# Ten bf16 conversions of a two-layer block move from ScalarE to GpSimd, in a hand-ordered attention loop

## Chip, cores and metric

The kernel runs on one core of one Trainium2 chip. The metric is the device time of one execution in microseconds (us). Work is spread over five engines that run their own instruction lists in order and meet only at semaphores: TensorE (PE in the profile, with its weight loads as PEld), VectorE (DVE), ScalarE (ACT), GpSimd (POOL) and SyncE (SP, which here only issues transfers).

## The reference, cut to what matters

```
x = x + tanh(g_xattn[0]) * L0_xattn(ctx, ctx, layernorm(x))     # long convolution
x = x + tanh(g_ffn[0])   * L0_ffn(layernorm(x))                 # dense + routed LoRA
x = x + tanh(g_xattn[1]) * L1_xattn(layernorm(x), ctx, ...)     # attention, 16 heads of 16
x = x + tanh(g_ffn[1])   * L1_ffn(layernorm(x), ...)            # 8 experts + shared one

def qdq(x):                                   # per row, to 8 bits and back
    s = max(max(abs(x), axis=-1) / 127, 1e-8)
    return clip(round(x / s), -127, 127) * s

def L1_xattn(x, cond, ...):
    q = qdq(x) @ qdq(wq).T + bq
    k, v = split(cond @ wkv.T + bkv)
    o = softmax(q k / sqrt(16)) v
    return qdq(o) @ qdq(wp).T + bp
```

x is 8 blocks of 128 rows by 256. The change concerns the third line alone, at the two places where a row is rounded (qdq(x) and qdq(o)).

## The kernel before, in words

Every engine has one list of instructions, written out by hand as loops over a stage number s. A block b is one of the 8 batches. The attention is a software pipeline of eight stages (s = 0 to 7) and a tail: in stage s the engines work on blocks s+3, s+2, s+1, s-1, s-2, s-3 and s-5 at different depths.

A row is rounded in two steps. VectorE multiplies by the reciprocal of the scale and adds 1.5 * 2^23, which leaves the integer in the low bits of the fp32 number. Then ScalarE subtracts that constant again and writes the small integer as bf16, which is exact. For the rows that go into the query projection the first step is the last one of `a_quant(b)` (line 1013, buffer AT_) and the second is `a_zq_(b)` (line 620, buffer AQ). For the attention outputs they are the last step of `o_norm(b)` (line 1055, buffer OT_) and `o_q_(b)` (line 661, buffer OQ).

What surrounds these two steps in a stage s, engine by engine, in the order of the lists:

- VectorE: maximum of the scores of block s (line 1022, two), the subtraction (line 1032, two), then `o_norm(s-2)` and `a_quant(s+3)` interleaved (lines 1042 to 1055 and 1002 to 1013), `m_rows(s-5)` (line 1073), `m_stats(s-4)` (line 1066).
- ScalarE: `a_zt_(s+2)` (line 624), exponential of quarter 0 of block s-1 (line 651), `m_rstd(s-5)` (lines 549 and 552), `o_q_(s-3)`, `a_q0_(s+2)` (line 630), exponential 1, `a_last_subtract(s)` (line 646, four), `a_q_(s+2)` (line 636), `a_rstd(s+3)` (lines 549 and 552), exponentials 2 and 3, `o_ev_(s-3)` (line 675), `a_zq_(s+3)`, `o_y_(s-3)` (line 670), `o_pe_(s-1)` (line 657), `m_zt_(s-5)` (line 685).
- TensorE: `a_turn(s-1, 0)` (line 1494), `a_transpose(s+2)` (line 1441), which waits for AQ and, for blocks 6 and 7, for `o_y_` of blocks 0 and 1, since both use PSUM bank 6; `o_rows(s-2)` (line 1519), `a_project(s+2)` (line 1447), `a_turn(s-1, 1)`, `a_q_transpose(s+2)` (line 1454), `a_turn(s-1, 2)` and `(s-1, 3)`, `a_scores(s+1)` (line 1480), which waits for the subtraction of block s on both engines, `o_transpose(s-3)` (line 1534), values (line 1510), `o_project(s-3)` (line 1540), values, `m_transpose(s-5)` (line 1587).
- GpSimd: for block b = 2 to 7 the masked keys of `block_keys(b)` (line 472, two), then, from b = 5, `finish(b-5)` (lines 482 and 484), which scales the attention's output and adds it to the residual. `finish` waits for `o_y_`. After block 7 come `finish(3)` and `finish(4)`. Blocks 5 to 7 are finished by VectorE.

After the attention the experts run: 16 units of matmuls (lines 1648 and 1666) with the transposing transfers of SyncE between them.

Of the kernel before, what the change touches and what calls it, by code (L numbers as in the profile page):

```python
# [23 lines left out]
ALU = mybir.AluOpType  # L24
# [5 lines left out]
NB = 8  # L30
# [12 lines left out]
ROUND = 1.5 * 2.0 ** 23  # L43
# [29 lines left out]
def build(nc, x, ctxr, kern, consts, rows, cols, wff, bt, wkv, wqp, gate, w1, w3, w2, sw1, sw3, sw2, out):  # L73
    with ExitStack() as ctx:
# [48 lines left out]
        def carve(region, at=0):  # L123
# [184 lines left out]
            "e_si",  # L308
            "e_ht",
            "e_acc"))  # L310
        e_xa, e_xd = sem("e_xa"), sem("e_xd")
        e_td = [sem("e_td%d" % n) for n in range(XS)]
        x4, stored = sem("x4"), sem("stored")
# [5 lines left out]
        AZT = 5  # L319
# [114 lines left out]
        @block.gpsimd  # L434
        def _(pool):
            nc.gpsimd.memset(ONES[:, :], 1.0).then_inc(ones_s, 1)
            nc.gpsimd.memset(EPSC[:, :], EPS).then_inc(ones_s, 1)
            nc.gpsimd.memset(GL[:, :, :], FULL).then_inc(ones_s, 1)
            pool.wait_ge(L["kern"], 16)
            nc.gpsimd.tensor_tensor(KP[:, P - 1:P], KP[:, P - 1:P], KP[:, 383:384], ALU.add).then_inc(lag0, 1)  # L440
            pool.wait_ge(L["ctx"], 16)
            for h in range(NH0):
                if not dve_has(h):
                    if h >= RING:
                        pool.wait_ge(conv, h - RING + 1)
                    if h == 3:
                        pool.wait_ge(nmr, 2)
                    upper(nc.gpsimd, h).then_inc(kv_p, 1)
                    lower(nc.gpsimd, h).then_inc(kv_p, 1)
            pool.wait_ge(conv, NH0)  # L450
            nc.gpsimd.memset(V[:, :, :, 16:17], 1.0).then_inc(v_ones, 1)
            nc.gpsimd.memset(V[:, :, :, 17:VW], 0.0).then_inc(v_ones, 1)

            def bias_values(b):

                pool.wait_ge(vev, b + 1)
                v = V[:, b, :, 0:HD1]
                nc.gpsimd.tensor_tensor(v, v, ROW[:, BV_AT:BV_AT + DM].rearrange("p (h d) -> p h d", h=NH1), ALU.add  # L458
                                        ).then_inc(v_b, 1)

            def block_keys(b):

                if b == 0:
                    pool.wait_ge(kev, 2)
                if b == GT:
                    pool.wait_ge(kev, 2 * NG)
                if b == 2:
                    pool.wait_ge(a_s0, 2)
                elif b > 2:
                    pool.wait_ge(a_s, b - 2)  # L470
                for c in range(2):
                    nc.gpsimd.tensor_tensor(KBD[:, b % 2, c], KT[:, c, b, :].unsqueeze(1).to_broadcast([P, 2, P]),  # L472
                                            MASK.unsqueeze(2).to_broadcast([P, 2, P]), ALU.mult).then_inc(kbd, 1)

            def bias_rows(b):
                pool.wait_ge(x2, b + 1)
                nc.gpsimd.tensor_tensor(XPB[:, b, :], X[:, b, :], BPG[:, :], ALU.add).then_inc(xpb, 1)

            def finish(b):

                pool.wait_ge(o_y, b + 1)
                nc.gpsimd.tensor_tensor(Y[:, b % 2, :], Y[:, b % 2, :], SWPB[:, :], ALU.mult).then_inc(o_sc, 1)  # L482
                pool.wait_ge(o_sc, b + 1)
                nc.gpsimd.tensor_tensor(X[:, b, :], Y[:, b % 2, :], XPB[:, b, :], ALU.add).then_inc(x3, 1)

            def expert_rows(u):

                g, e = divmod(u, NE)
                pool.wait_ge(m_gt, gates_done(g))
                if u == 0:  # L490
                    pool.wait_ge(a_et, 4 * NB)
                if u >= XS:
                    pool.wait_ge(e_td[u % XS], 16 * (u // XS))
                for j in range(2):
                    b = GT * g + j
                    nc.gpsimd.tensor_scalar(XB[:, u % XS, j, :], MX[:, b, :], GG[:, b, e:e + 1], 1.0,  # L496
                                            ALU.mult, ALU.mult).then_inc(e_xb, 1)


            def fold_sums(b):  # L500

                pool.wait_ge(prod, 3 * NH0)
                pair = PR[:, :, :, :, :].rearrange("p (a b) i h j -> p b a (i h j)", a=NL)[:, b]
                nc.gpsimd.tensor_tensor(pair[:, :, 0:512], pair[:, :, 0:512], pair[:, :, 512:1024], ALU.add  # L504
                                        ).then_inc(fold, 1)

            fold_sums(FOLD0)
            bias_values(0)
            fold_sums(FOLD0 + 1)
            for b in range(1, NB - 2):  # L510
                bias_values(b)
                if b + FOLD0 + 1 < NB:
                    fold_sums(b + FOLD0 + 1)
            pool.wait_ge(prep, PREP)
            pool.wait_ge(isum, NB)
            block_keys(0)
            bias_values(NB - 2)
            bias_values(NB - 1)
            block_keys(1)
            for b in range(NB - 2):  # L520
                bias_rows(b)
            pool.wait_ge(v_dg, 3)
            for b in range(2, NB):
                block_keys(b)
                if b < 4:
                    bias_rows(b + NB - 4)
                if b >= 5:
                    finish(b - 5)
            for b in range(NB - 5, NB - LATE):
                finish(b)  # L530
            expert_rows(0)
            expert_rows(1)
            for u in range(2, NG * NE):
                expert_rows(u)

        @block.scalar
        def _(act):
# [120 lines left out]

            def o_q_(b):
                act.wait_ge(o_n, ONT * (b + 1))  # L660
                nc.scalar.activation(OQ[:, b % 2, :], OT_[:, b % 2, :], ACT.Copy, bias=-ROUND).then_inc(o_q, 1)

            def o_y_(b):
# [61 lines left out]
            for s in range(NB):  # L725
                if s + 2 < NB:
                    a_zt_(s + 2)
                if s >= 1:
                    a_exp(s - 1, 0)
                if s >= 5:  # L730
                    m_rstd(s - 5)
                if s >= 3:
                    o_q_(s - 3)
                if s + 2 < NB:
                    a_q0_(s + 2)
                if s >= 1:
                    a_exp(s - 1, 1)
                a_last_subtract(s)
                if s + 2 < NB:
                    a_q_(s + 2)  # L740
                if 1 <= s < NB - 3:
                    a_rstd(s + 3)
                if s >= 1:
                    a_exp(s - 1, 2)
                    a_exp(s - 1, 3)
                if s >= 3:
                    o_ev_(s - 3)
                if s + 3 < NB:
                    a_zq_(s + 3)
                if s >= 3:  # L750
                    o_y_(s - 3)
                if s >= 1:
                    o_pe_(s - 1)
                if s >= 5:
                    m_zt_(s - 5)
# [66 lines left out]
        def _(dve):  # L822
# [173 lines left out]
            def a_quant(b, k):  # L996

                a, s = b % 2, s_az
                s.wait()
                if k == 0:  # L1000
                    dve.wait_ge(a_rs, 2 * (b + 1))
                    s.mark(V_.tensor_scalar(AZ[:, a, :], X[:, b, :], MV[:, b, 0:1], RS[:, b:b + 1],
                                            ALU.subtract, ALU.mult))
                elif k == 1:
                    s.mark(V_.tensor_reduce(AM[:, b:b + 1], AZ[:, a, :], AX.X, ALU.max, apply_absolute_value=True))
                elif k == 2:
                    s.mark(V_.tensor_scalar(AS[:, b:b + 1], AM[:, b:b + 1], 1.0 / QMAX, SMIN, ALU.mult, ALU.max))
                elif k == 3:
                    s.mark(V_.reciprocal(AR[:, b:b + 1], AS[:, b:b + 1]))
                else:  # L1010
                    if b >= 2:
                        dve.wait_ge(a_zq, b - 1)
                    s.mark(V_.tensor_scalar(AT_[:, a, :], AZ[:, a, :], AR[:, b:b + 1], ROUND, ALU.mult, ALU.add))

# [20 lines left out]
            def o_norm(b, k):  # L1035
# [14 lines left out]
                elif k == 4:  # L1050
                    s.mark(V_.reciprocal(OR[:, b:b + 1], OS[:, b:b + 1]))
                else:
                    if b >= 2:
                        dve.wait_ge(o_q, b - 1)
                    s.mark(V_.tensor_scalar(OT_[:, a, :], O[:, a, :], OR[:, b:b + 1], ROUND, ALU.mult, ALU.add))


# [227 lines left out]
        def _(pe):  # L1285
# [148 lines left out]


            def a_transpose(b):
                pe.wait_ge(a_zq, b + 1)
                chain_free(b - 2)
                for k in range(NL):
                    at = 64 * k  # L1440
# [79 lines left out]
                ins.then_inc(o_nt, 1)  # L1520

            def o_transpose(b):
                pe.wait_ge(o_q, b + 1)
                if b + 5 < NB:
                    pe.wait_ge(a_q, 2 * (b + 6))
                elif b < NB - LATE:
# [234 lines left out]
```

## Time and profile before

| | |
|---|---|
| median of 3 runs | 219.73 us (219.03 to 220.08) |
| profiled execution, time | 218.84 us |
| profiled execution, span | 216.7 us, so 2.14 us lie around the span |
| mean granted TensorE clock | 0.965 |
| busy in the span: PE, DVE, ACT, POOL | 176.3, 164.2, 108.5, 81.5 us |

The span is what the profiler sees between the first and the last instruction; the time of a run also holds what lies around it. The attention loop takes from about 105 to 163 us of the span.

### The profile page before, as it was taken

How to read it: one execution, taken by the hardware profiler on the slowest of the kernel's cores; microseconds unless marked ns; L12 is line 12 of the kernel's file. 1: busy time of each engine (PE TensorE's matmuls, PEld its weight loads, DVE VectorE, ACT ScalarE, POOL GpSimd, SP SyncE). 2: the span in 40 equal slices, each digit the busy share in tenths (PEclk: the TensorE clock that was granted, in tenths of full speed). 3: DMA queues.
4: the chain of work that ended last, by engine and by line, in shares of the span. 5: the costliest groups of instructions: out<-in, count | busy, mean ns of one | idle time of the engine just before them, and what ended most of it. 6: DMA issues, size and time to landing. Idle time of an engine off the chain costs nothing.

```text
span 216.7 us, 3606 instructions
## 1 busy us (share of the span) xinstructions
PE 176.3 (81%) x1156; PEld 111.4 (51%) x1156; DVE 164.2 (76%) x465; ACT 108.5 (50%) x288; POOL 81.5 (38%) x114
## 2 busy tenths in 40 slices
PE   0369999989989989885788788798787959979962
PEld 0236555558555556542455556565566327636531
DVE  0698999994178999979689999999936853575634
ACT  2440343211423245641588789887975473543621
POOL 1386557024755550593121204420220373065100
PEclk9999999999999999999599999999999788999998
DMA  6989970000000000000000000000000057665772
GB/s 182 395 208 374 363 258 15 3 0 0 0 0 2 3 0 2 0 0 2 3 0 0 5 0 5 3 0 0 3 0 3 2 97 145 76 120 113 161 164 97
DMA packets 22625, 15.17 MB, mean 70 GB/s; under 512 B 17648, under 2 KB 21328, under 8 KB 22096
## 3 DMA queue, kind: packets, MB, share of 16 engines
q1 hardware_dynamic: 21968, 13.94, 24.1%
q10 hardware_dynamic: 640, 1.02, 1.3%
q8 instruction: 9, 0.15, 0.3%
q14 instruction: 8, 0.07, 0.1%
HBM read 9.68 MB, written 1.07 MB: 50 GB/s over the span
## 4 chain that ended last, share of the span: by engine, by line
PE 50%; DVE 18%; ACT 12%; DMA 7%; issue 7%; SPq 4%; DVEq 0%
PE PS L1648 7%; PE PS L1316 5%; PE PS L1318 5%; PE PS L1317 5%; DMA X<-x 4%; PE PS L1404 4%; PE PS L1666 3%; PE PS L1380 3%; DMA R<-R 3%; SPq L426 3%; PE PS L1338 3%; ACT R L651 3%; ACT R L646 2%; PE PS L1480 2%; PE PS L1347 2%
## 5 line engine op out<-in xcount | busy, mean ns | idle before, releaser
L496 POOL TENSOR_SCALAR R<-QT,SM 128x256 bf16<-128x256 f32 x32 | 15.8, 508 | 28.0 <-DVE SM L1100 19.6
L1269 DVE TENSOR_TENSOR R<-R,PS 128x512 bf16<-128x512 f32 (+1 forms) x17 | 11.7, 687 | 15.4 <-ACT R L773 8.1
L1022 DVE TENSOR_REDUCE SM<-PS 128x8 f32<-128x1024 f32 x16 | 18.8, 1213 | 3.0 <-PE PS L1480 1.9
L1648 PE MATMUL PS<-R 128*128 128x512 bf16 x64 | 17.1, 388 | 3.6 <-DMA R<-R 3.6
L1494 PE MATMUL PS<-CON,R 128*128 128x128 f32 x128 | 19.0, 281 | 1.2 <-ACT R L651 1.2
L472 POOL TENSOR_TENSOR R<-R,CON 128x256 f32<-128x256 f32 x16 | 9.6, 620 | 24.7 <-PE PS L1480 15.5
L651 ACT ACTIVATE R<-PS 128x512 f32<-128x512 f32 x32 | 18.4, 600 | 0.9 <-PE PS L1494 0.8
L337 POOL TENSOR_TENSOR R<-CT 128x512 f32<-128x512 f32 x12 | 13.8, 1154 | 12.2 <-PE PS L1318 6.7
L773 ACT ACTIVATE R<-PS 128x512 f32<-128x512 f32 x17 | 10.1, 596 | 14.8 <-PE PS L1648 14.8
L549 ACT ACTIVATE LNV<-MV,EPSC 128x1 f32<-128x1 f32 (+1 forms) x26 | 7.6, 293 | 17.6 <-DVE MV L945 11.2
L1494 PEld LDWEIGHTS PS<-CON,R 128*128 128x128 f32 x128 | 14.5, 143 | 3.5 <-issue 3.0
L1316 PE MATMUL PS<-R,T_R 128*128 128x384 f32 x32 | 13.8, 514 | 2.1 <-DVE T_R L837 2.1
L1666 PE MATMUL PS<-R 128*128 128x256 bf16 (+1 forms) x80 | 14.5, 309 | 0.2 <-DVE R L1257 0.2
L1032 DVE TENSOR_TENSOR R<-PS,SM 128x1024 f32<-128x1024 f32 (+1 forms) x16 | 14.6, 947 | 0.0
L482 POOL TENSOR_TENSOR T_R<-T_R,SWPB 128x256 f32<-128x256 f32 x5 | 3.6, 728 | 27.9 <-ACT T_R L670 27.9
L504 POOL TENSOR_TENSOR R<-R 128x1024 f32<-128x1024 f32 x6 | 14.1, 2353 | 0.0
L1317 PE MATMUL PS<-R,T_R 128*128 128x384 f32 x32 | 13.6, 509 | 0.0
L1318 PE MATMUL PS<-R,T_R 128*128 128x384 f32 x32 | 13.6, 509 | 0.0
L1404 PE MATMUL PS<-WFF,T_R 128*128 128x352 f32 x32 | 11.4, 480 | 2.5 <-ACT T_R L600 2.1
L1666 PEld LDWEIGHTS PS<-R 128*128 128x128 bf16 (+1 forms) x80 | 10.0, 127 | 6.0 <-DVE R L1269 1.4
L570 ACT CAST R<-WST 128x2048 bf16<-128x2048 f32 x3 | 5.7, 1900 | 12.9 <-DMA WST<-w 12.9
L458 POOL TENSOR_TENSOR R<-R,ROW 128x256 f32<-128x256 f32 x8 | 6.1, 767 | 15.1 <-ACT R L591 15.0
(152 smaller groups left out, 428.1 us busy)
## 6 DMA issues: line engine op xcount, KB each, us to landing
WST<-w SPq DMA_DIRECT2D x3, 1024.0 KB, 11.3
T_R<-lagged SPq DMA_DIRECT2D x2, 768.0 KB, 7.7
X<-x SPq DMA_DIRECT2D x2, 512.0 KB, 6.9
CT<-ctxr SPq DMA_DIRECT2D x1, 1024.0 KB, 7.5
y<-X SPq DMA_DIRECT2D x8, 128.0 KB, 1.9
WKV<-wkv SPq DMA_DIRECT2D x1, 512.0 KB, 9.9
WQP<-wqp ACTq DMA_DIRECT2D x1, 512.0 KB, 6.2
R<-sw SPq DMA_DIRECT2D x3, 128.0 KB, 4.4
```

The source lines that it names most:

```text
L496: nc.gpsimd.tensor_scalar(XB[:, u % XS, j, :], MX[:, b, :], GG[:, b, e:e + 1], 1.0, ALU.mult, ALU.mult).then_inc(e_xb, 1)
L504: nc.gpsimd.tensor_tensor(pair[:, :, 0:512], pair[:, :, 0:512], pair[:, :, 512:1024], ALU.add).then_inc(fold, 1)
L651: nc.scalar.activation(ET[:, b % 2, 4 * k:4 * k + 4, :], PS[:, 4 + k % 2, :].rearrange("p (h n) -> p h n", h=4), ACT.Exp).then_inc(a_ex, 1)
L1022: V_.tensor_reduce(MX1[:, b % 2, 8 * c:8 * c + 8], S4[:, 8 * c:8 * c + 8, :], AX.X, ALU.max, negate=True).then_inc(a_mx, 1)
L1032: V_.tensor_tensor(SS[:, a, ks, :], S4[:, ks, :], MX1[:, a, ks].unsqueeze(2).to_broadcast([P, n, P]), ALU.add).then_inc(a_sub, 1)
L1316: M(one, T[:, h, 0:P], kv[:, 0:NB], start=True, stop=True)
L1317: M(two, T[:, h, P:2 * P], kv[:, 0:NB], start=True, stop=False)
L1318: M(two, T[:, h, 0:P], kv[:, NB:2 * NB], start=False, stop=True).then_inc(conv, 1)
L1404: ins = M(PS[:, 6 + b % 2, 0:352], FZT[:, b % 2, k, :], WFF[:, k, :], start=(k == 0), stop=(k == NL - 1))
L1494: ins = TR(PS[:, 4 + k % 2, P * h:P * h + P], SS[:, b % 2, 4 * k + h, :], I)
L1648: ins = M(PS[:, 2 + 2 * (v % 2) + n, :], lhs, rhs, start=(k == 0), stop=(k == NL - 1))
L1666: ins = M(acc(g, j), src[:, P * j:P * j + P], W2[:, e - 1, :] if e >= 1 else SW2, start=(e == 0 and j % 2 == 0), stop=(e == NE), skip_grou ...
```

## The change

GpSimd gets two new steps. `rounded_rows(b)` does for blocks 3 to 7 what `a_zq_(b)` did, and `rounded_out(b)` for blocks 0 to 4 what `o_q_(b)` did: the same subtraction of the constant with bf16 output, as a `tensor_scalar`. Two semaphores, a_zp and o_qp, count them; the waits of VectorE (buffer free again) and TensorE (rows ready) follow. ScalarE keeps the rows of blocks 0 to 2 and the outputs of blocks 5 to 7.

```diff
+            def rounded_rows(b):
+
+                pool.wait_ge(a_z, AZT * (b + 1))
+                pool.wait_ge(a_tr, b - 1)
+                nc.gpsimd.tensor_scalar(AQ[:, b % 2, :], AT_[:, b % 2, :], -ROUND, None, ALU.add).then_inc(a_zp, 1)
+
+            def rounded_out(b):
+
+                pool.wait_ge(o_n, ONT * (b + 1))
+                if b >= 2:
+                    pool.wait_ge(o_tr, b - 1)
+                nc.gpsimd.tensor_scalar(OQ[:, b % 2, :], OT_[:, b % 2, :], -ROUND, None, ALU.add).then_inc(o_qp, 1)
...
             for b in range(2, NB):
+                if b >= 3:
+                    rounded_rows(b)
+                if b >= 5:
+                    rounded_out(b - 5)
                 block_keys(b)
                 if b < 4:
                     bias_rows(b + NB - 4)
                 if b >= 5:
                     finish(b - 5)
             for b in range(NB - 5, NB - LATE):
+                rounded_out(b)
                 finish(b)
...
             def o_q_(b):
                 act.wait_ge(o_n, ONT * (b + 1))
+                if b == NB - LATE:
+                    act.wait_ge(o_tr, b - 1)
...
-                if s >= 3:
-                    o_q_(s - 3)
                 if s + 2 < NB:
                     a_q0_(s + 2)
...
-                if s + 3 < NB:
-                    a_zq_(s + 3)
                 if s >= 3:
                     o_y_(s - 3)
...
-                    if b >= 2:
+                    if b >= 5:
+                        dve.wait_ge(a_zp, b - 4)
+                    elif b >= 2:
                         dve.wait_ge(a_zq, b - 1)
...
-                    if b >= 2:
-                        dve.wait_ge(o_q, b - 1)
+                    if b == NB - 1:
+                        dve.wait_ge(o_q, 1)
+                    elif b >= 2:
+                        dve.wait_ge(o_qp, b - 1)
...
             def a_transpose(b):
-                pe.wait_ge(a_zq, b + 1)
+                if b < 3:
+                    pe.wait_ge(a_zq, b + 1)
+                else:
+                    pe.wait_ge(a_zp, b - 2)
...
             def o_transpose(b):
-                pe.wait_ge(o_q, b + 1)
+                if b < NB - LATE:
+                    pe.wait_ge(o_qp, b + 1)
+                else:
+                    pe.wait_ge(o_q, b - (NB - LATE) + 1)
```

The first place is GpSimd's list from the keys of block 5 on. Before, it reads as follows (line 472 the keys, 482 and 484 `finish` of blocks 0 and 1; in brackets the semaphores that a row waits for):

```order
L472 TENSOR_TENSOR R<-R,CON 128x256 [waits a_s]
L472 TENSOR_TENSOR R<-R,CON 128x256
L482 TENSOR_TENSOR T_R<-T_R,SWPB 128x256 [waits o_y]
L484 TENSOR_TENSOR X<-T_R,R 128x256 [waits o_sc]
L472 TENSOR_TENSOR R<-R,CON 128x256 [waits a_s]
```

In the changed kernel the same stretch holds the new steps (line 491 `rounded_rows`, 498 `rounded_out`; 473, 483 and 485 are the old 472, 482 and 484). It begins with the rows of block 5:

```order
L491 TENSOR_SCALAR R<-R 128x256 [waits a_tr,a_z]
L498 TENSOR_SCALAR R<-R 128x256 [waits o_n]
L473 TENSOR_TENSOR R<-R,CON 128x256 [waits a_s]
L473 TENSOR_TENSOR R<-R,CON 128x256
L483 TENSOR_TENSOR T_R<-T_R,SWPB 128x256 [waits o_y]
L485 TENSOR_TENSOR X<-T_R,R 128x256 [waits o_sc]
L491 TENSOR_SCALAR R<-R 128x256 [waits a_tr,a_z]
L498 TENSOR_SCALAR R<-R 128x256 [waits o_n]
```

The last two rows are the rows of block 6 and the outputs of block 1. They stand behind `finish(0)`, which waits for ScalarE's `o_y_(0)`. In the same way the rows of block 7 stand behind `finish(1)`.

The second place is ScalarE's list at the end of stage 4 and the start of stage 5. Before (line 675 `o_ev_(1)`, 620 `a_zq_(7)`, 670 `o_y_(1)`, 657 `o_pe_(3)`, 624 `a_zt_(7)`, 651 exponential 0 of block 4, 549 and 552 `m_rstd(0)`, 661 `o_q_(2)`, 630 `a_q0_(7)`):

```order
L675 COPY R<-PS 128x256 [waits o_tr]
L620 ACTIVATE R<-R 128x256 [waits a_z]
L670 ACTIVATE T_R<-PS,SM 128x256 [waits o_mm]
L657 COPY T_R<-PS 128x512 [waits a_pv]
L624 COPY R<-PS 128x256 [waits a_tr]
L651 ACTIVATE R<-PS 128x512 [waits a_et]
L549 ACTIVATE LNV<-MV,EPSC 128x1 [waits m_ln]
L552 ACTIVATE RS<-LNV 128x1 [waits m_rs]
L661 ACTIVATE R<-R 128x256 [waits o_n]
L630 ACTIVATE T_R<-PS,SM 128x256 [waits a_mm]
```

In the changed kernel (the line numbers are 18 to 21 higher):

```order
L696 COPY R<-PS 128x256 [waits o_tr]
L691 ACTIVATE T_R<-PS,SM 128x256 [waits o_mm]
L676 COPY T_R<-PS 128x512 [waits a_pv]
L643 COPY R<-PS 128x256 [waits a_tr]
L670 ACTIVATE R<-PS 128x512 [waits a_et]
L568 ACTIVATE LNV<-MV,EPSC 128x1 [waits m_ln]
L571 ACTIVATE RS<-LNV 128x1 [waits m_rs]
L649 ACTIVATE T_R<-PS,SM 128x256 [waits a_mm]
```

The two conversions, old lines 620 and 661, are gone from between the others, and with the first of them ScalarE's wait for VectorE's a_z.

## Rows read from the trace of the kernel before

**Rows 1.** Page, part 1: busy time, share of the span and instructions by engine.

```profile
PE 176.3 (81%) x1156; PEld 111.4 (51%) x1156; DVE 164.2 (76%) x465; ACT 108.5 (50%) x288; POOL 81.5 (38%) x114
```

**Rows 2.** Windows of stages 4, 5, 7: length; busy PE, PEld, DVE, ACT, POOL.

```profile
129.70:137.20 7.50, 6.26 (x85) 4.42 (x78) 7.43 (x20) 6.62 (x19) 2.61 (x4) 1.00 0.01 3
137.20:143.80 6.60, 5.34 (x68) 3.88 (x60) 6.43 (x14) 6.44 (x19) 2.60 (x4) 1.00 0.01 2
...
150.40:157.00 6.60, 5.07 (x75) 3.64 (x72) 6.43 (x14) 5.72 (x16) 1.46 (x2) 1.00 0.01 2
```

**Rows 3.** Chain that ended last, in order of time: start, length, what.

```profile
136.96 0.35 DVE R L1013
137.33 0.42 ACT R L620
...
146.91 0.40 ACT R L661
...
153.75 0.40 ACT R L661
```

**Rows 4.** Timeline of ScalarE: start, length, instruction, idle time ahead and its releaser.

```profile
129.78 0.42 ACT L620 ACTIVATE R<-R 128x256 bf16<-128x256 f32 x1 [0.98 <-DVE R L1013]
130.10 0.46 ACT L670 ACTIVATE T_R<-PS,SM 128x256 f32<-128x256 f32 x1
...
134.99 0.20 ACT L552 ACTIVATE RS<-LNV 128x1 f32<-128x1 f32 x1
...
139.65 0.20 ACT L552 ACTIVATE RS<-LNV 128x1 f32<-128x1 f32 x1
139.76 0.40 ACT L661 ACTIVATE R<-R 128x256 bf16<-128x256 f32 x1
```

**Rows 5.** Timeline of GpSimd.

```profile
120.33 1.23 POOL L472 TENSOR_TENSOR R<-R,CON 128x256 f32<-128x256 f32 x2 [5.65 <-PE PS L1480]
130.64 0.73 POOL L482 TENSOR_TENSOR T_R<-T_R,SWPB 128x256 f32<-128x256 f32 x1 [9.08 <-ACT T_R L670]
131.44 0.74 POOL L484 TENSOR_TENSOR X<-T_R,R 128x256 f32<-128x256 f32 x1
132.14 1.19 POOL L472 TENSOR_TENSOR R<-R,CON 128x256 f32<-128x256 f32 x2
```

**Rows 6.** Timeline of TensorE.

```profile
128.86 0.39 PE L1540 MATMUL PS<-R 128*128 128x256 bf16 x2 [0.21 <-ACT R L675]
...
130.70 0.27 PE L1441 MATMUL PS<-IDB,R 128*128 128x128 bf16 x2 [0.29 <-ACT T_R L670]
...
134.22 1.15 PE L1480 MATMUL PS<-R 32*128 32x256 f32 x16 [0.30 <-ACT R L646]
...
136.48 0.39 PE L1540 MATMUL PS<-R 128*128 128x256 bf16 x2 [0.33 <-ACT R L675]
...
138.25 0.27 PE L1441 MATMUL PS<-IDB,R 128*128 128x128 bf16 x2 [0.22 <-ACT T_R L670]
```

**Rows 7.** Timeline of VectorE.

```profile
120.35 0.75 DVE L1002 TENSOR_SCALAR R<-X,MV,RS 128x256 f32<-128x256 f32 x1
...
135.30 0.41 DVE L1002 TENSOR_SCALAR R<-X,MV,RS 128x256 f32<-128x256 f32 x1
```

**Rows 8.** Groups by line: the GpSimd conversion to bf16 in the experts.

```profile
L496 POOL TENSOR_SCALAR R<-QT,SM 128x256 bf16<-128x256 f32 x32 | 15.8, 508 | 28.0 <-DVE SM L1100 19.6 <-DMA R<-R 8.4
```

**Rows 9.** Timeline of TensorE: longest idle times after 20 us, scores of block 1.

```profile
101.17 0.30 PE L1410 MATMUL PS<-CON,T_R 128*64 128x128 f32 x1 [1.43 <-DVE T_R L977]
...
105.61 2.09 PE L1480 MATMUL PS<-R 32*128 32x256 f32 x16 [0.44 <-ACT R L646]
...
175.51 0.44 PE L1587 MATMUL PS<-CON,QT 128*128 128x128 f32 x2 [1.48 <-DVE QT L1073]
```

**Rows 10.** Windows behind them: the granted clock is the third number from the end.

```profile
103.00:104.00 1.00, 0.61 (x2) 0.13 (x2) 1.00 (x3) 0.30 (x2) 0.00 (x0) 0.50 0.00 0
...
178.00:179.00 1.00, 1.00 (x5) 0.58 (x3) 0.00 (x0) 0.70 (x3) 0.80 (x2) 0.50 0.00 0
```

More of the change, by code:

```diff
@@ L310, in build @@
             "e_acc"))
+        a_zp, o_qp = sem("a_zp"), sem("o_qp")
         e_xa, e_xd = sem("e_xa"), sem("e_xd")
```

## Prediction

> **What bounds the kernel now.** I read the page first, then windows by stage, then the chain that ended last, then the timelines of each engine from 120 to 160 us. The page alone misleads: ScalarE is busy for half of the span only [rows 1]. But in the attention loop nearly everything is full. In stage 4 VectorE is busy 7.43 of 7.50 us, and in stage 5 ScalarE and VectorE are both busy 6.4 of 6.6 us [rows 2]. The chain shows a hand-over inside this loop. Up to 137.3 us it runs along VectorE, the last piece being the rounding of block 7 (line 1013). At 137.33 it goes to ScalarE's conversion of the same rows, and from there to the end of the attention it alternates between ScalarE and TensorE; the conversions of outputs are pieces of it at 146.91 and 153.75 [rows 3], and the one at 139.76 lies on it as well [rows 4]. So ScalarE's conversions cost something only from stage 4's end on. Before that VectorE sets the pace and ScalarE waits for it: 0.98 us ahead of the conversion of block 6 [rows 4].
>
> **What the change removes.** Five conversions of 0.42 us (rows) and five of about 0.40 us (outputs) leave ScalarE, some 4.1 us of busy time. Instructions overlap a little there: a conversion started at 129.78 and its follower at 130.10, so one is worth 0.32 us of ScalarE's time [rows 4]. On the chain lie the outputs of blocks 2, 3 and 4, three times 0.31 (139.76 follows at 0.11 after the line before, whose result it does not need), hence **0.93 us given back**, if nothing else moves. The conversion of block 7 is on the chain too, but its work does not go away: TensorE still waits for it, now from GpSimd.
>
> **What it adds.** Ten conversions on GpSimd. The trace has no GpSimd conversion with a constant. The nearest row is the experts' one-input operation of the same shape and output type, 0.51 us [rows 8]. Its lower bound is ScalarE's own 0.42 [rows 4], its upper bound the two-input operation of 0.73 [rows 5]. I take 0.50. By the first of these a conversion is 0.1 us slower than today, which alone is nothing.
>
> **The order on GpSimd is the costly part.** The rows of block 6 stand behind `finish(0)`, and those of block 7 behind `finish(1)`. `finish(0)` waits for ScalarE's `o_y_(0)`, today started at 130.10 with 0.46 us [rows 4], and GpSimd's two operations of it step from 130.64 to 131.44 to about 132.14, that is 1.50 us [rows 5]. TensorE takes the rows of block 6 at 130.70 and those of block 7 at 138.25 [rows 6]. I follow the new order:
>
> 1. `o_y_(0)` no longer stands behind a conversion that waits for VectorE. It can start when `o_project(0)` is done. That is at 128.86 + 0.39 today [rows 6]. TensorE's steps of stage 3 come some 0.4 us earlier: VectorE wins 0.33 us (below), and ScalarE has one 0.31 us operation less ahead of them. So `o_y_(0)` starts at 128.9, ends at 129.3, `finish(0)` runs from 129.4 to 130.9, and the rows of block 6 are ready at 130.9 + 0.50 = 131.4. TensorE starts at 131.45 instead of 130.70: **0.75 us late**, with its queue stopped: `o_rows(2)`, `a_project(6)`, the transposes of block 3 and the scores of block 5 all stand behind it.
> 2. ScalarE needs 0.12 us less on the way from there to the scores of block 5, because o_q_(1) is gone and the rest waits for TensorE. The scores start 0.62 late, 134.84 instead of 134.22, and `o_project(1)` 0.63 late, 137.11 instead of 136.48 [rows 6]. `o_y_(1)` starts at its end, 137.5; it ends at 138.0, `finish(1)` at 139.6, the rows of block 7 at 140.1. TensorE takes them at 140.13 instead of 138.25: **1.88 us late**.
> 3. From there the chain of before repeats at its later place and gets the three operations back: 1.88 - 0.31 = 1.57 at the scores of block 6, 1.26 at those of block 7, 0.95 at the end of stage 7. No conversion leaves ScalarE after this, so the tail and the experts start **1.0 us later**.
>
> The delay is not repeated after block 7, since only conversions of outputs stand behind `finish(2)` and `finish(3)`, and TensorE wants those late in the stage.
>
> **VectorE's account.** In stage 4 its step at 135.30 needs `a_rstd(7)`, which ended at 134.99 + 0.20 [rows 4, 7]. That now ends near 135.8, so VectorE waits about 0.9 us; in stage 5 it waits again for the late scores, about 0.6. Both lie beside the delay of the chain (it is 1.57 late there against VectorE's 1.2) and add nothing. One term is a gain: at 120.35 line 1002 took 0.75 us, while GpSimd had started the keys of block 5 at 120.33; at 135.30 the same instruction took 0.41 with GpSimd idle [rows 5, 7]. In the new order the keys of block 5 wait behind the rows of block 5 until about 123, so these 0.33 us come back in stage 2, and step 1 has used them.
>
> Whether the ten new operations slow VectorE in the same way is the other side of that row. I place them: rows follow directly on VectorE's line 1013, and outputs follow on rows, so both meet VectorE's maximum and subtraction, which read PSUM; at 132.14 keys ran beside these [rows 5] in a stage that was full without a lengthened step. I count nothing. If all ten met a step such as line 1002, it would be 10 times 0.33, 3.3 us of VectorE's time. The Trainium skill, page "SBUF — State Buffer", section "SBUF: two separate sides", says that GpSimd and some VectorE operations share one pair of ports as an exclusive lock, held for a whole instruction. The row at 120.35 agrees for one meeting. By that rule alone every meeting with such an operation would cost, a loss of up to those 3.3 us; by the placement from the rows the sum has none.
>
> **Sum.** 0.75 late at block 6, 1.88 at block 7, less 0.93: +0.95, call it +1.0 us. The profiled execution of before took 218.84 us, of which 216.7 are span, so the changed one's like is 219.8 with a span near 217.7. Its median of three is 0.89 above that execution, 219.73, so I forecast **220.7 us** (+0.45%). With GpSimd's conversion at 0.42 or 0.73 the two delays change by -0.08 and +0.23 each, which gives +0.8 to +1.4; the hand-followed steps of ScalarE and TensorE may be 0.3 off on either side. This case's own range is 220.2 to 221.5.
>
> **Rivals.**
> - *TensorE's clock falls in the new gaps* (28%). The two waits make idle times of about 1.5 us, from 130.0 and from 138.7. After 20 us the trace has two idle times as long, 1.43 and 1.48 us, and within two to three microseconds of each the granted clock was 0.50, the 1.2 GHz level, where it had been 1.00 [rows 9, 10]. At 0.50 the 16 score matmuls took 2.09 us [rows 9], at 1.00 they took 1.15 [rows 6]. Against it: in stage 4 TensorE is dense on both sides of the gap (6.26 of 7.50 us busy [rows 2]). Price: +0.94 for the scores and about as much for the transposes ahead of them, 1.8 us per fall, one or two falls: 1.0 + 1.8 = +2.8, or +4.6, that is 222.5 to 224.3.
> - *The delay is taken up and the saving stays, faster* (15%). One mechanism: `o_y_(1)` starts early enough. The end is no later than today when the rows of block 7 come at most 0.93 us late, so TensorE's start at 139.18, so `o_y_(1)` ended by 137.1, where I have 138.0. For it speaks that today it waits for VectorE's a_z (chain at 137.33 [rows 3]) and that ScalarE idles in stages 2 to 4; against it that `o_project(1)` started only at 136.48 even with TensorE on time [rows 6]. With no delay at all the gain would be 0.93, plus 0.33 from VectorE: 218.5. Less delay gives something between 218.5 and 219.7.
> - *Nothing to be seen* (12%): rows of block 6 late by less than I have, because VectorE's end of stage 3 also moves, and both accounts cancel: 219.4 to 220.2.
> - My forecast has 45%.
>
> **From cases to numbers.** Between kernels of this length about 0.5%, 1.1 us, can be told from no change. The forecast's case lies across that bound, half on each side: 0.22 same, 0.23 slower. The clock adds 0.27 to slower. The early `o_y_` gives 0.12 faster and 0.03 same, the cancelling case 0.12 same. Together faster 0.12, same 0.38, slower 0.50. The range leaves out the far end of the clock's case and the full gain: 218.9 to 223.5.
>
> **What the next profile should show.** Right: TensorE's line for `a_transpose` waits for GpSimd with one idle time near 1.5 us at 130 and one at 139 us; `finish(0)` starts near 129.4 and `finish(1)` near 138.1, each directly ahead of a conversion; VectorE idles at `a_quant(7)` for `a_rstd(7)`; scores of block 6 start near 143.8, the attention ends about 1 us later than now; GpSimd's conversion near 0.5 us. Wrong: no wait of TensorE for GpSimd, or the block-7 rows ready before 139.2. A granted clock below 1.00 between 130 and 150 us would be the first rival. What would upset the whole is a wait that I did not follow, above all on GpSimd ahead of keys or outputs.

## The result, and the profile after

The changed kernel took 222.64 us (median of 4, 222.30 to 222.93) against 219.91 us for the kernel before: ratio 1.014, 95% interval 1.010 to 1.018. It is slower, by more than the likeliest case of the forecast and within the forecast's range. The ratios of this document leave out executions that took over 1.5% more than the fastest of the same kernel. The profiled execution took 222.65 us with a span of 220.6 us, 3.9 us more than before.

The page's busy times first (it is the line that answers to [rows 1]):

```profile
PE 179.9 (82%) x1156; PEld 114.5 (52%) x1156; DVE 163.4 (74%) x465; ACT 106.4 (48%) x278; POOL 90.1 (41%) x124
```

ScalarE has ten instructions less and is busy for 2.1 us less, but GpSimd has 8.6 us more for ten conversions, 0.86 us each. TensorE has the same number of instructions and is busy 3.6 us longer; its mean granted clock fell from 0.965 to 0.942.

Windows of stages 4 and 5, cut where VectorE starts its maximum, and one from the start of stage 7 to about the end of the attention, to set beside [rows 2] (the third number from the end is the mean granted clock):

```profile
129.90:139.60 9.70, 7.78 (x94) 5.69 (x82) 7.45 (x20) 6.46 (x18) 4.24 (x6) 0.82 0.01 2
139.60:148.80 9.20, 6.91 (x56) 4.84 (x44) 6.54 (x15) 5.60 (x16) 4.23 (x6) 0.73 0.01 3
...
156.00:163.00 7.00, 5.78 (x86) 4.04 (x88) 6.51 (x13) 5.53 (x16) 2.29 (x3) 1.00 0.01 2
```

Stages 4 and 5 took 9.7 and 9.2 us where they had taken 7.5 and 6.6, with the same work for VectorE (7.45 and 6.54 us) and a mean granted clock of 0.82 and 0.73 in place of 1.00. That is 4.8 us. Stage 6 adds 0.66 (7.23 us from 148.78 to 156.01, against 6.57 from 143.81 to 150.38), and 0.19 was there already: VectorE began stage 4 at 129.85 instead of 129.66. Stage 7 adds nothing.

GpSimd's timeline, the answer to [rows 5] (lines 483 and 485 are `finish`, 491 the rows, 498 the outputs):

```profile
130.28 0.73 POOL L483 TENSOR_TENSOR T_R<-T_R,SWPB 128x256 f32<-128x256 f32 x1 [4.72 <-ACT T_R L691]
131.08 0.72 POOL L485 TENSOR_TENSOR X<-T_R,R 128x256 f32<-128x256 f32 x1
131.77 0.85 POOL L491 TENSOR_SCALAR R<-R 128x256 bf16<-128x256 f32 x1
...
139.87 0.72 POOL L483 TENSOR_TENSOR T_R<-T_R,SWPB 128x256 f32<-128x256 f32 x1 [5.29 <-ACT T_R L691]
140.68 0.72 POOL L485 TENSOR_TENSOR X<-T_R,R 128x256 f32<-128x256 f32 x1
141.37 0.85 POOL L491 TENSOR_SCALAR R<-R 128x256 bf16<-128x256 f32 x1
```

TensorE's, the answer to [rows 6] (1465 `a_transpose`, 1504 the scores, 1614 `m_transpose(2)`, the first work of TensorE behind stage 7's values):

```profile
132.68 0.28 PE L1465 MATMUL PS<-IDB,R 128*128 128x128 bf16 x2 [1.83 <-POOL R L491]
...
136.88 1.16 PE L1504 MATMUL PS<-R 32*128 32x256 f32 x16
...
142.27 0.28 PE L1465 MATMUL PS<-IDB,R 128*128 128x128 bf16 x2 [1.82 <-POOL R L491]
...
146.62 2.09 PE L1504 MATMUL PS<-R 32*128 32x256 f32 x16
...
163.54 0.41 PE L1614 MATMUL PS<-CON,QT 128*128 128x128 f32 x2
```

The same hand-over shows twice: `finish` starts when ScalarE's `o_y_` is done, the rows begin directly behind it, and TensorE, idle for 1.83 and 1.82 us, starts 0.05 us after them. VectorE had finished its part of block 6 at 129.93, so its rows stood ready for GpSimd 1.84 us before GpSimd took them up at 131.77. The 16 score matmuls take 1.16 us behind the first wait and 2.09 us behind the second.

VectorE's timeline, the answer to [rows 7] (1019 is the old 1002):

```profile
120.86 0.41 DVE L1019 TENSOR_SCALAR R<-X,MV,RS 128x256 f32<-128x256 f32 x1
...
137.71 0.41 DVE L1019 TENSOR_SCALAR R<-X,MV,RS 128x256 f32<-128x256 f32 x1 [2.18 <-ACT RS L571]
...
148.78 2.36 DVE L1041 TENSOR_REDUCE SM<-PS 128x8 f32<-128x1024 f32 x2 [2.48 <-PE PS L1504]
```

The lengthened step of [rows 7], 0.75 us, is gone: 0.41. VectorE, which had no idle time in these stages, now waits 2.18 and 2.48 us.

Windows of one microsecond for the granted clock, as in [rows 10]:

```profile
134.00:135.00 1.00, 1.00 (x6) 0.89 (x5) 0.97 (x5) 0.62 (x2) 0.59 (x2) 0.50 0.00 0
...
137.00:138.00 1.00, 1.00 (x17) 0.62 (x18) 0.29 (x1) 0.97 (x5) 0.00 (x0) 1.00 0.00 0
...
144.00:145.00 1.00, 0.70 (x4) 0.70 (x5) 0.96 (x3) 1.00 (x4) 0.18 (x1) 0.50 0.07 16
...
149.00:150.00 1.00, 1.00 (x18) 0.58 (x18) 1.00 (x2) 0.37 (x1) 0.00 (x0) 0.50 0.00 0
```

Behind each of the two idle times TensorE runs at the 1.2 GHz level for a while, called a fall below: once between 133 and 137 us, once between 143 and 151, so the second fall lasts about twice as long. At the end of the attention the changed kernel is 5.53 us late (163.54 against 158.01), but the span grew by 3.9 only. Most of the rest is a fall that the profiled execution of before had later and this one had not. Before, then after, over the same stretch:

```profile
167.00:171.00 4.00, 3.86 (x9) 1.70 (x8) 3.62 (x22) 1.75 (x6) 0.00 (x0) 0.57 0.01 2
```

```profile
167.00:171.00 4.00, 2.98 (x50) 2.33 (x50) 2.42 (x10) 2.99 (x9) 0.00 (x0) 1.00 0.02 4
```

The first group of the experts' matmuls, in this fall before the change and outside it after:

```profile
167.81 3.31 PE L1648 MATMUL PS<-CT,R 128*128 128x512 f32 x4
```

```profile
173.12 1.88 PE L1675 MATMUL PS<-CT,R 128*128 128x512 f32 x4
```

### The profile page after: what moved, and what is told of

It is laid out like the page before. It is cut to its first block, busy times and chain, and to the rows that moved or that the text cites. A ratio compares the mean times of both kernels' runs of the same rounds, so it can differ in the third digit from the quotient of the medians.

```text
span 220.6 us, 3615 instructions
## 1 busy us (share of the span) xinstructions
PE 179.9 (82%) x1156; PEld 114.5 (52%) x1156; DVE 163.4 (74%) x465; ACT 106.4 (48%) x278; POOL 90.1 (41%) x124
## 2 busy tenths in 40 slices
DMA packets 22625, 15.17 MB, mean 69 GB/s; under 512 B 17648, under 2 KB 21328, under 8 KB 22096
## 3 DMA queue, kind: packets, MB, share of 16 engines
q10 hardware_dynamic: 640, 1.02, 1.2%
HBM read 9.68 MB, written 1.07 MB: 49 GB/s over the span
## 4 chain that ended last, share of the span: by engine, by line
PE 51%; DVE 16%; ACT 13%; DMA 7%; issue 6%; SPq 3%; POOL 3%; DVEq 0%; ACTq 0%; POOLq 0%
PE PS L1337 5%; PE PS L1675 5%; PE PS L1339 5%; PE PS L1338 5%; DMA X<-x 4%; PE PS L1425 4%; ACT R L670 3%; PE PS L1693 3%; DMA R<-R 3%; ACT R L665 3%; PE PS L1401 3%; PE PS L1359 3%; PE PS L1518 3%; PE PS L1504 2%; PE PS L1534 2%
## 5 line engine op out<-in xcount | busy, mean ns | idle before, releaser
L510 POOL TENSOR_SCALAR R<-QT,SM 128x256 bf16<-128x256 f32 x32 | 16.4, 528 | 25.7 <-DVE SM L1121 19.3
L1518 PE MATMUL PS<-CON,R 128*128 128x128 f32 x128 | 22.5, 318 | 0.5 <-ACT R L670 0.5
L1518 PEld LDWEIGHTS PS<-CON,R 128*128 128x128 f32 x128 | 17.8, 165 | 2.9 <-issue 2.4
L1693 PE MATMUL PS<-R 128*128 128x256 bf16 (+1 forms) x80 | 13.9, 300 | 0.7 <-DVE R L1290 0.5
L1693 PEld LDWEIGHTS PS<-R 128*128 128x128 bf16 (+1 forms) x80 | 9.5, 121 | 6.6 <-DVE R L1290 2.4
```

The lines of the kernel that those rows point to most:

```text
L1518: ins = TR(PS[:, 4 + k % 2, P * h:P * h + P], SS[:, b % 2, 4 * k + h, :], I)
L1693: ins = M(acc(g, j), src[:, P * j:P * j + P], W2[:, e - 1, :] if e >= 1 else SW2, start=(e == 0 and j % 2 == 0), stop=(e == NE), skip_grou ...
```

## The experiments

Three theories were put against each other: Q, the place of the rows behind `finish` in GpSimd's queue; S, the conversion itself, slow on GpSimd; C, the clock that falls in the new idle times. All ratios are to the kernel before, measured on the same chip, and kernels are told apart by intervals in TensorE's timeline of the profiled execution, which hold no fall from elsewhere: from taking the rows of block 6 to taking those of block 7, and from there to `m_transpose(2)`. A third, from block 3 to block 5, shows what happens ahead of them. The table at the end has them for every kernel that was timed repeatedly.

**e1_order: rows ahead of finish.**

```diff
-                if b >= 3:
+                if 3 <= b <= 5:
                     rounded_rows(b)
...
+                if 5 <= b <= 6:
+                    rounded_rows(b + 1)
                 if b >= 5:
                     finish(b - 5)
```

> The changed kernel with one thing different: on GpSimd the rows of blocks 6 and 7 stand ahead of finish(0) and finish(1), not behind them. Theory Q (the place in GpSimd's queue made the loss): TensorE takes the rows of block 6 at 130.9 and of block 7 at 138.2, as early as before the change within 0.3 us, no idle time there is over 1.0 us, no clock fall between 130 and 150 us, and ScalarE's three saved conversions show: 219.0 us, 0.9 less than before the change. Rival S (the GpSimd conversion itself, 0.85 us instead of ScalarE's 0.42, is what costs): each handover stays 0.4 to 0.8 us late whatever the order, 220.3 to 221.5 us.

Measured: 218.69 us, ratio 0.995 (0.991 to 0.998). GpSimd and TensorE in stages 4 and 5:

```profile
130.71 0.85 POOL L491 TENSOR_SCALAR R<-R 128x256 bf16<-128x256 f32 x1 [4.48 <-DVE R L1034]
131.52 0.73 POOL L483 TENSOR_TENSOR T_R<-T_R,SWPB 128x256 f32<-128x256 f32 x1
...
138.22 0.85 POOL L491 TENSOR_SCALAR R<-R 128x256 bf16<-128x256 f32 x1 [3.18 <-DVE R L1034]
```

```profile
131.61 0.29 PE L1467 MATMUL PS<-IDB,R 128*128 128x128 bf16 x2
...
139.12 0.29 PE L1467 MATMUL PS<-IDB,R 128*128 128x128 bf16 x2 [0.30 <-POOL R L491]
```

GpSimd now waits for VectorE ahead of the rows, as it should, and TensorE waits 0.30 us where it had waited 1.82. (The times are about 1 us later than Q's 130.9 and 138.2: this execution was at half clock from 100 us on, that of before from 102 us, and took the rows of block 2 at 103.71 instead of 102.45, ahead of everything that the change touches.) From block 6 to 7 it takes 7.51 us, as before the change. Moving two conversions turns a loss of 1.4% into a gain of 0.5%, with the slow conversion still in place. Q had said 219.0, S 220.3 to 221.5.

**e3_outs: only the outputs move.** Rows are again converted by ScalarE (`a_zq_` and its waits as before), `rounded_out` stays.

```diff
-                if b >= 3:
-                    rounded_rows(b)
                 if b >= 5:
                     rounded_out(b - 5)
...
+                if s + 3 < NB:
+                    a_zq_(s + 3)
                 if s >= 3:
                     o_y_(s - 3)
```

> Only the attention outputs of blocks 0 to 4 go to GpSimd; all rows are converted by ScalarE as before the change. Theory Q: no conversion that TensorE waits for early in a stage is on GpSimd, so only the saving of three times 0.31 us is left: 219.0 us, 0.9 less than before. Rival S: a 0.85 us conversion ahead of o_transpose shows as a wait of TensorE at that line and the time is no better than before, 219.7 to 220.5 us.

Measured: 218.05 us, ratio 0.995 (0.992 to 0.999). Its line 1460 is `a_transpose(7)` here, 1609 `m_transpose(2)`; the second fence is the kernel before:

```profile
137.69 0.27 PE L1460 MATMUL PS<-IDB,R 128*128 128x128 bf16 x2 [0.22 <-ACT T_R L689]
...
156.52 0.41 PE L1609 MATMUL PS<-CON,QT 128*128 128x128 f32 x2
```

```profile
158.01 0.41 PE L1587 MATMUL PS<-CON,QT 128*128 128x128 f32 x2
```

18.83 us from block 7's rows to `m_transpose(2)`, against 158.01 - 138.25 = 19.76 before: 0.93 us, the three conversions of 0.31 us of the forecast. In the attention's timeline no transpose of outputs waits for GpSimd.

**e8_rows_only: only the rows move**, in the changed order; `o_q_` is back on ScalarE for all blocks.

```diff
-                if b >= 5:
-                    rounded_out(b - 5)
...
             for b in range(NB - 5, NB - LATE):
-                rounded_out(b)
                 finish(b)
...
+                if s >= 3:
+                    o_q_(s - 3)
```

> The other half alone: rows of blocks 3 to 7 on GpSimd in the changed kernel's order, outputs back on ScalarE. Theory: the two halves add. The change cost 1.2 to 1.4% and the outputs alone gained 0.5%, so the rows alone cost 1.7 to 2.1%, ratio 1.017 to 1.021, with TensorE's two waits for GpSimd of about 1.8 us in stages 4 and 5. Rival (the outputs on GpSimd were part of the loss, by the queue they share): less than the whole change, ratio 1.005 to 1.012.

Measured: 224.33 us, ratio 1.023 (1.018 to 1.028). With the outputs' 0.995 that makes 1.018, and the whole change has 1.014 (1.010 to 1.018): the halves add within their intervals, the rows carry the loss, and the outputs in the same queue are no part of it. Block 7's rows to `m_transpose(2)` take 22.18 us against 21.27 of the change, 0.91 more: the three conversions again. TensorE's wait at block 6 is as long as in the change:

```profile
132.12 0.28 PE L1460 MATMUL PS<-IDB,R 128*128 128x128 bf16 x2 [1.82 <-POOL R L491]
```

**e7_rows35: rows of blocks 6 and 7 back to ScalarE**, the rest as changed.

```diff
-                if b >= 3:
+                if 3 <= b < 6:
                     rounded_rows(b)
...
+                if s + 3 in (6, 7):
+                    a_zq_(s + 3)
```

> The changed kernel with only the rows of blocks 6 and 7 given back to ScalarE; rows of blocks 3 to 5 and the outputs of blocks 0 to 4 stay on GpSimd in the slow form. Theory Q (all the loss enters at blocks 6 and 7, behind finish): as fast as e3_outs within 0.3%, ratio 0.994 to 0.998. Rival S (every conversion of rows on GpSimd costs, and five are moved): three fifths of the loss stay, ratio 1.006 to 1.010.

Measured: 217.82 us, ratio 0.993 (0.989 to 0.996), as e3_outs within the intervals. The loss against the kernel before enters at the two blocks whose rows stand behind `finish`. The other three rows are not quite free: from block 3 to block 5 TensorE takes 14.52 us in e1_order and e2_fill, with rows on GpSimd at 0.85 us, and 14.10 in e3_outs, where ScalarE converts them. Against the kernel before most of that 0.42 us is hidden by the 0.33 that the later keys give back. (e7_rows35 itself shows 15.17, because its execution, like that of the changed kernel, was at half clock until 112 to 113 us and not only until about 110.)

**e2_fill: work in TensorE's idle times.** In stages 4 and 5 the four transposes of `o_rows`, whose input is ready, are done three more times ahead of the wait, into the same bank and with the same values.

```diff
+                if s in (4, 5):
+                    for _ in range(3):
+                        o_rows(s - 2, False)
                 if s + 2 < NB:
                     a_transpose(s + 2)
```

> The changed kernel, with work put into TensorE's two idle times: in stages 4 and 5 the four transposes of o_rows are done three times more, without a signal, ahead of the wait for GpSimd's rows (they write the same values to a bank nobody reads yet). All waits for GpSimd stay. Theory C (a part of the loss is the granted clock that falls after the two idle times): clock stays at 1.00 from 130 to 150 us, scores of block 6 take 1.15 us instead of 2.09, and the time falls by 2.0 to 2.5 us against the changed kernel, to 220.1 to 220.7 us. Rival Q alone (only the waits count, the falls lie beside them): within 0.5 us of the changed kernel, 222.6 us.

Measured: 220.09 us, ratio 1.003 (1.000 to 1.006), against 1.014 for the change. TensorE does 24 transposes more and the attention ends earlier:

```profile
132.10 0.28 PE L1465 MATMUL PS<-IDB,R 128*128 128x128 bf16 x2 [0.18 <-POOL R L491]
...
141.13 0.28 PE L1465 MATMUL PS<-IDB,R 128*128 128x128 bf16 x2 [0.18 <-POOL R L491]
...
144.77 1.15 PE L1504 MATMUL PS<-R 32*128 32x256 f32 x16 [0.30 <-ACT R L665]
...
159.91 0.41 PE L1615 MATMUL PS<-CON,QT 128*128 128x128 f32 x2
```

Over 130 to 150 us the granted clock is 1.00. The rows of block 6 come as late behind VectorE's rounding as in the change (2.74 us against 2.75), but the scores of block 6 take 1.15 us again. From block 7's rows to `m_transpose(2)` it is 18.78 us instead of 21.27: the second fall cost 2.49 us. From block 6 to 7 it is 9.03 instead of 9.59: the first cost 0.56. What is left, 9.03 against 7.55 before, 1.48 us, is the wait itself. In the medians the filling is worth 2.5 us, the upper end of C's 2.0 to 2.5; Q alone had allowed 0.5.

**e4_forms: four ways to write the conversion.** The order of e1_order, one execution (219.43 us), so each of the four is one row. The expression differs from block to block (shortened):

```diff
+  if b == 4:    tensor_scalar(AQ, AT_, -ROUND, 1.0, ALU.add, ALU.mult)
+  elif b == 5:  tensor_scalar(AQ, AT_, NEGR[:, 0:1], None, ALU.add)
+  elif b == 6:  tensor_scalar(AQ, AT_, NEGR[:, 0:1], 1.0, ALU.add, ALU.mult)
+  else:         tensor_scalar(AQ, AT_, -ROUND, None, ALU.add)
```

> As e1_order, but the GpSimd conversion of the rows is written in four ways to price it: blocks 3 and 7 add a constant alone, as in the change (0.85 us); block 4 adds a constant and then multiplies by 1.0; block 5 adds a per-row value from a tile; block 6 adds the per-row value and multiplies by 1.0. Theory F (the operation's form sets the price, as the experts' multiply by a per-row value and 1.0 takes 0.53 us at the same shape and types): at least one of the other three is under 0.6 us. Rival (the price is that of the data, or of an addition): all are within 0.05 us of 0.85.

GpSimd's timeline, blocks 3, 4, 5 and 6:

```profile
106.56 0.86 POOL L501 TENSOR_SCALAR R<-R 128x256 bf16<-128x256 f32 x1 [4.32 <-issue]
...
116.08 0.41 POOL L495 TENSOR_SCALAR R<-R 128x256 bf16<-128x256 f32 x1 [5.27 <-issue]
...
123.37 0.92 POOL L497 TENSOR_SCALAR R<-R,NEGR 128x256 bf16<-128x256 f32 x1 [5.74 <-issue]
...
130.76 0.48 POOL L499 TENSOR_SCALAR R<-R,NEGR 128x256 bf16<-128x256 f32 x1 [4.50 <-issue]
```

With one operation 0.86 and 0.92 us, with two 0.41 and 0.48. A multiplication by 1.0 more halves the time; a per-row value in place of the constant adds 0.06 to 0.07 us. It is the form with two operations that [rows 8] had priced: the experts multiply by a per-row value and by 1.0.

**e5_two_op: the change with the two-operation form**, order untouched (shortened).

```diff
-  nc.gpsimd.tensor_scalar(AQ[:, b % 2, :], AT_[:, b % 2, :], -ROUND, None, ALU.add)
+  nc.gpsimd.tensor_scalar(AQ[:, b % 2, :], AT_[:, b % 2, :], -ROUND, 1.0, ALU.add, ALU.mult)
```

(and the same for the outputs)

> The changed kernel, its order untouched, with the ten GpSimd conversions written as add the constant, then multiply by 1.0 (0.41 us in e4_forms, against 0.85 for the addition alone). Theory Q with the size of the operation in it: rows still come behind finish(0) and finish(1), each 0.44 us sooner, so TensorE's two waits shrink from 1.8 to 1.3 to 1.4 us and the lateness at block 7 from 4.0 to about 2 us with falls of the clock in some executions: 220.5 to 221.5 us, ratio 1.005 to 1.010. Rival S (the duration was all): no slower than before the change, ratio 0.995 to 1.000.

Measured: 219.48 us, ratio 1.000 (0.997 to 1.004). By its time that is the upper end of what S had said (0.995 to 1.000) and less than Q's 1.005 to 1.010. The profiled execution was its longest, 221.47 us, which the ratio leaves out; it has one fall in these stages, behind the first wait:

```profile
131.87 0.40 PE L1465 MATMUL PS<-IDB,R 128*128 128x128 bf16 x2 [1.38 <-POOL R L491]
...
136.21 1.15 PE L1504 MATMUL PS<-R 32*128 32x256 f32 x16 [0.22 <-ACT R L665]
...
141.40 0.28 PE L1465 MATMUL PS<-IDB,R 128*128 128x128 bf16 x2 [1.38 <-POOL R L491]
```

```profile
132.00:133.00 1.00, 1.00 (x7) 0.93 (x6) 1.00 (x2) 0.70 (x2) 1.00 (x3) 0.50 0.00 0
```

Q had the waits right, 1.38 us each. The second wait of 1.38 us was not followed by a fall here: 18.84 us from block 7's rows to `m_transpose(2)`. So the form of the operation was worth 1.4% in this order, more than its own 0.44 us at two waits: 2.43 us of it are the second fall, which did not come (18.84 us against 21.27).

**e9_two_op_fill: e5 with the idle times filled** (two repetitions of `o_rows` in place of three).

> e5_two_op (the changed order, conversions in the two-operation form) with o_rows' four transposes done twice more in TensorE's idle times of 1.38 us in stages 4 and 5. e5 had a fall of the clock at 132 us in its profiled execution and times from 218.0 to 221.5 us. Theory C (in e5 some executions fall and some don't, and the fast ones show the waits alone): no fall between 125 and 150 us, ratio to before 0.993 to 0.998. Rival (the falls were no longer worth anything there): 1.000 as e5.

Measured: 220.30 us, ratio 1.006 (1.003 to 1.010). A miss: it is not faster than e5 but by its ratio slower (the intervals just touch), though in the profile the filled kernel has no fall between 125 and 150 us, and from block 6 to block 7 it takes 8.59 us against 9.53:

```profile
132.66 0.29 PE L1465 MATMUL PS<-IDB,R 128*128 128x128 bf16 x2 [0.17 <-POOL R L491]
...
141.25 0.29 PE L1465 MATMUL PS<-IDB,R 128*128 128x128 bf16 x2 [0.17 <-POOL R L491]
```

Neither theory holds: C had said 0.993 to 0.998, the rival 1.000. This profile ran at 0.50 in stretches from 100, 168.6 and 178.9 us, outside these stages; the first of them puts block 2's rows at 103.70 instead of e5's 102.29. From there to `m_transpose(2)` it is 1.6 us faster than e5's profile (56.33 against 57.95 us). So the filling works where it stands, and why the time does not follow stays open. e5's one profile was its slowest of ten executions, and no trace shows whether the others had a fall to take away. Nor was it tested whether the falls outside move with the filling; the two kernels also ran on different chips.

**e6_order_two_op: both remedies**, the order of e1_order and the form of e5_two_op.

> Both remedies: rows of blocks 6 and 7 ahead of finish(0) and finish(1), and the two-operation form. Theory Q: rows are now ready before TensorE asks in stages 4 and 5, and its remaining waits at that line, 1.5 us in three places in e1_order, go below 0.5: ratio to before 0.988 to 0.993, 0.4 to 1.2 us less than e1_order. Rival (VectorE and the ScalarE chain set the pace again, the rows were early enough): the same as e1_order, ratio 0.995.

Measured: 216.72 us, ratio 0.990 (0.986 to 0.994), the fastest version found, faster than both kernels. (One of its eleven executions took 932 us; no trace shows why, and the ratio leaves it out.)

```profile
129.36 0.40 POOL L491 TENSOR_SCALAR R<-R 128x256 bf16<-128x256 f32 x1 [5.37 <-DVE R L1034]
```

```profile
129.82 0.29 PE L1467 MATMUL PS<-IDB,R 128*128 128x128 bf16 x2
...
137.33 0.29 PE L1467 MATMUL PS<-IDB,R 128*128 128x128 bf16 x2
```

The conversion starts when VectorE is done, and in stages 4 and 5 TensorE no longer waits for GpSimd. Of the waits for rows one is left, 0.47 us for block 5, where e1_order had 0.49, 0.67 and 0.30. Q said below 0.5.

| kernel | ratio | block 3 to 5 | block 6 to 7 | block 7 to m_transpose(2) |
|---|---|---|---|---|
| before | 1 | 14.42 | 7.55 | 19.76 |
| changed | 1.014 | 15.17 | 9.59 | 21.27 |
| e1_order | 0.995 | 14.52 | 7.51 | 18.84 |
| e2_fill | 1.003 | 14.52 | 9.03 | 18.78 |
| e3_outs | 0.995 | 14.10 | 7.53 | 18.83 |
| e5_two_op | 1.000 | 14.72 | 9.53 | 18.84 |
| e6_order_two_op | 0.990 | 14.08 | 7.51 | 19.00 |
| e7_rows35 | 0.993 | 15.17 | 7.53 | 18.83 |
| e8_rows_only | 1.023 | 14.53 | 9.55 | 22.18 |
| e9_two_op_fill | 1.006 | 14.08 | 8.59 | 18.78 |

The last two intervals (in us) repeat to 0.25 us among kernels that share the cause, e5's 9.53 apart, which is a shorter wait and a fall behind it. The first holds three things: 0.33 less where the keys no longer meet VectorE's step (every kernel but before), 0.42 to 0.45 more where the rows take 0.85 us on GpSimd (changed, e1, e2, e7, e8), and 0.65 more in the three executions whose early stretch at half clock went on for 3 us or more behind block 3's rows (changed, e5, e7). The ratios don't always follow the intervals, by some tenths of a per cent; falls elsewhere differ from profile to profile.

## Why the prediction was right, and where it was off

- **Direction and place: right.** The rows of blocks 6 and 7 stand behind `finish(0)` and `finish(1)`, TensorE idles there, and VectorE then at `a_quant(7)`. e1_order and e7_rows35 remove just this and the loss is gone.
- **The saving of 0.93 us: right**, 0.92 or 0.93 in e1, e3, e5 and e7 (19.76 less 18.83 or 18.84), 0.98 in e2 and e9, 0.76 in e6. The 4.1 us of busy time that were to leave ScalarE are 2.1 on the page, where overlapping instructions count once; no term of the sum used them.
- **The 0.33 us of the keys: right.** Line 1019 took 0.41 us at 120.86. From block 3 to block 5 e3, e6 and e9 take 14.08 to 14.10 us against 14.42 before: 0.32 to 0.34 less. In e3 only the outputs have moved, and the keys of block 5 start at 122.18. That the added operations would not slow VectorE is right too: in stage 4 its work is 7.45 us against 7.43 [rows 2], with six GpSimd operations beside it.
- **The price of the conversion: wrong.** The step took 0.50 us from [rows 8], with 0.73 as the upper end. It is 0.85. The row was of the same shape and types but of two operations, and the form is what sets the price (e4_forms). From VectorE's rounding of block 6 done to TensorE's start there are 132.68 - 129.93 = 2.75 us, before 130.70 - 129.75 = 0.95. The forecast had 131.45 - 129.42 = 2.03, so 0.72 are missing. e9, in the same order with 0.40 in place of 0.85, has 132.66 - 130.61 = 2.05: 0.70 less for 0.45 of price. It enters once in full, by the rows of block 6 themselves, and a second time in part (0.25), by those of block 5, which hold up ScalarE's way to `o_y_(0)`. For the 0.35 by which the price was missed that gives, as an estimate, 0.54 of the 0.72. The rest lies in the steps followed.
- **The likeliest case: wrong.** The clock's fall was the first rival, at 28%, against 45% for the forecast's own case without one. It came behind both waits, and 0.56 + 2.49 = 3.05 us went to it, against 1.8 us a fall in the forecast: the first was priced three times too high, the second, which lasted twice as long, too low. The step that failed is the argument from density, that work on both sides of the gap would hold the clock. With waits of 1.83 and 1.82 us it did not, in either stage; with the two of 1.38 us in e5_two_op it fell once and once not. The trace of before had one more fall to show, at 167 us behind a wait of 1.02 us, which the forecast did not list.
- **That the time lies in the range: in part luck.** The rival's number for two falls was 224.3 us, outside the range of 218.9 to 223.5; two falls came, and the measured 222.64 is its number for one. What came back behind the attention is the next point but one.
- **The sum, in terms:** 1.98 us late at block 6 (forecast 0.75), 2.04 more at block 7 (1.13; 1.48 of wait and 0.56 of clock), then 1.51 more (forecast 0.93 less): 5.53 us at the end of the attention. Of the 1.98 about 0.6 belong to the execution and not to the change: it stayed at half clock until 113 us, that of before until about 110. e2_fill, whose list is the same up to there, stayed so until 110 as well and takes block 6 at 132.10, 1.40 late.
- **From 5.53 us to the measured time.** The span is 3.9 us longer, the median 2.7. 1.4 us came back by the fall at 167 us, which the profiled execution of before had: its first four matmuls of the experts take 3.31 us where the changed kernel's take 1.88. The same 1.02 us wait stands ahead of them in all eleven profiles, and a fall follows in four of them (before, e5, e7, e9), so I take it for luck of an execution. The profiled execution of before was also 1.07 us under its median, which accounts for the step from 3.9 to 2.7; what the others of its executions had in its place no trace shows, and it stays open.

## What to carry to other kernels

Work moved to an idle engine's queue waits for whatever stands ahead of it: find what that instruction waits for, here ScalarE's output of the same stage, and put the moved work ahead of it when its own input comes first. A stall that seems small should be priced twice, by its length and by what TensorE's clock does behind it; here work put into the idle time saved 2.5 us in one kernel and nothing in another, so it has to be timed. Take an operation's price from a row of the same form, with the same number of operations, not only of the same shape and types.

## What was not expected of the hardware

- On GpSimd a `tensor_scalar` of 128x256 from fp32 to bf16 took 0.85 us with one operation and 0.41 us with two (add, then multiply by 1.0); with a per-row value 0.92 and 0.48 (these two from one row each).
- Idle times of TensorE of 1.82 and 1.83 us between dense stretches were each followed by a granted clock of 0.50, the 1.2 GHz level, two in the changed kernel and two in e8_rows_only; the 16 score matmuls behind the second of each took 2.09 us instead of 1.15. Of two idle times of 1.38 us in e5_two_op one was, and of eleven of 1.02 us at the same place, one in each profile, four.
